# Where the work of a two-layer graph kernel stands: adjacency maxima out of the second sweep, a new order in the gates' stage, filters read once

## The chip, the cores and the metric

The kernel runs on one core of a Trainium2 chip. The metric is the device time of one execution in microseconds (us), lower is better. Its engines are PE (TensorE matmul, with weight loads listed apart as PEld), DVE (VectorE), ACT (ScalarE), POOL (GpSimd) and SP (SyncE, which issues all DMAs here). Each has its own instruction queue, worked in order; semaphores tie them together.

## The reference, cut to what matters

There are 64 graphs, each with 256 nodes of 256 channels, and a 256x256 adjacency of zeros and ones.

```python
h = relu(layernorm(x))
# layer 0, with xc = transpose(h)
c = relu(bn1(conv1d(xc, conv1_w)))                 # 1 tap
x_conv = relu(bn2(conv1d(c, conv2_w, pad=8)) + xc)  # 17 taps, 256 x 256 channels
s = h @ w_se.T + b_se                               # 3 values a node
A = exp(-|s_n - s_m|^2) * adj
x_nmp = A @ relu(h @ w_msg.T + b_msg)
gi = concat(x_conv, x_nmp) @ w_ih.T + b_ih ; gh = h @ w_hh.T + b_hh
r, z = sigmoid(gi_r + gh_r), sigmoid(gi_z + gh_z)
x1 = x + (1 - z) * tanh(gi_n + r * gh_n) + z * h
# layer 1, with h2 = relu(layernorm(x1))
out = x1 + relu(h2 @ W[:256] + (adj @ h2) @ W[256:] + bias)
```

## The kernel before

All matmuls of the main work take float16 operands, each value split in a high and a low part and multiplied in three passes. ACT makes the high part, DVE the low one. The splits need powers of two as scales, which come from the largest values and norms of the inputs. The convolution of 17 taps is done in the frequency domain. The kernel has four stages, one after another.

**Preparation** (`convolution_weights`). The filters of `conv2_w` become spectra. They are read twice: once as `conv2_w` (two DMAs of 2176 KB into `wnat`) for the norm of each output channel, L350 on DVE and L321 on ACT, and once as `conv2_tiles`, 37 tiles of 7 output channels, each tile a block of 119 partitions (channel in the tile, tap) by 256 (three DMAs, `CHUNKS`, L251). The first tile DMA waits for the first half of `wnat`, the second for the other half. Once all norms are there, a tile is scaled and split (even pairs of tiles by ACT L316 and DVE L357, odd pairs by POOL L304 to L309), multiplied on PE (L467, 6 matmuls), and its spectrum is split from PSUM into SBUF by ACT (L335) and DVE (L430).

**First sweep** (`convolution`, 66 slots `q`). A slot takes the graphs through a pipeline: DVE takes statistics (L989) and normalises (L1001), PE turns (L1219), ACT and DVE split (L904, L1007), PE multiplies with `conv1_w` (L1230), DVE adds the bias (L1017), ACT and DVE split (L911, L1022), PE transforms (L1244), ACT and DVE split the spectrum (L922, L1029). SP loads an `x` and stores `x_normed` and `h_turned`. In slots 1 to 11 ACT also negates a block of filters (L934), and SP stores the filters in slots 0 to 11 (`store_filters`). From slot 18 on three quarters of a main unit are worked in as well: a unit is 12 matmuls of 512 columns (L1271), a split by ACT (L928) and DVE (L1034) into one of three buffers `ysb`, and a store of 256 KB (L710).

**Second sweep** (same function, 60 units `u`). The main units only, three PSUM banks and three `ysb` buffers deep. Around them, at fixed `u`: all 64 adjacencies are loaded by SP (L761, `load_adj`, 256 KB each, two buffers in `xin`) and reduced to their maxima by DVE (L1070, `adj_max`) by the plan `ADJ_AT`; filters are loaded again and negated (u below 14); two loads of 3072 KB bring spectra back (L738, `load_bins`, before the loop and at u = 11); `place_sides` and `turn_sides` at u = 26 to 36; the weights of the gates are loaded at u = 36 (L765 to L771), squared, summed, scaled and split.

**Gates** (`gates`, 65 slots of one graph). PE runs, for graph t: `distances`, `messages`, `first_h(0)`, `first_conv_rz(0)`, `weighted`, `first_conv_n(0)`, `inverse(t+1)`, `gates_second(0)`, then `turn2(t-1)`, `first_h(1)`, `layer1(t-1)`, `first_conv_rz(1)`, `first_conv_n(1)`, `neighbours(t-1)`, `gates_second(1)`. Nearly all of these are L1557. DVE, ACT and POOL follow in hand-written orders. `weighted_low` (DVE L1649) releases `gates_second(0)`; `norm2` (DVE L1760) releases `turn2` (PE L1771); `finish` adds and rectifies the output.

In the code below, `then` waits for the instruction that it wraps.

## Time and profile before

| what | value |
|---|---|
| median of 3 runs | 1932.36 us (1928.71 to 1933.15) |
| the profiled execution's own time | 1935.05 us |
| its span | 1932.8 us |
| PE busy | 1785.4 us, 92% |
| DVE busy | 1531.6 us, 79% |
| ACT busy | 841.0 us, 44% |
| DMA | 245.55 MB, mean 127 GB/s |
| chain that ended last | PE 36%, DVE 23%, ACT 5% |

Busy shares are means over stages with different limits, so the stages have to be read one at a time. "Idle before" in a row is time in which the engine of that row stood still, with what ended it.

### The profile page before, as it was taken

What the parts mean: (1) busy time and instruction counts of PE and PEld (TensorE: products, weight loads), DVE (VectorE), ACT (ScalarE), POOL (GpSimd) and SP (SyncE); (2) the same over time, 40 slices, a digit from 0 to 9 for tenths busy, and PEclk for the clock granted to TensorE, in tenths of its full rate; (3) what the DMA queues carried; (4) which work ended last, traced back from release to release, by engine and by line L of the source; (5) the groups of instructions that cost most, each with busy time, mean ns of one, the idle gap of its engine ahead of it and who ended that gap; (6) DMA issues with size and microseconds to landing.
All of it is one profiled execution on the core that took longest, in us unless ns stands there. A gap on an engine that the chain in (4) does not pass through costs nothing.

```text
span 1932.8 us, 36810 instructions
## 1 busy us (share of the span) xinstructions
PE 1785.4 (92%) x12477; PEld 1167.3 (60%) x12478; DVE 1531.6 (79%) x3386; ACT 841.0 (44%) x1489; POOL 439.1 (23%) x616
## 2 busy tenths in 40 slices
PE   2778999977779999999999999999999999999997
PEld 1566777732334666666666666666666666666664
DVE  4899999944544788888888888888888888888886
ACT  3664544432233444444444444444444444444442
POOL 3521111100001222222222222222222222222221
PEclk9899999998989999999999999999999999999998
DMA  6376676578684223222232222322223222232320
GB/s 190 108 277 231 220 267 201 193 261 278 190 276 138 76 73 100 79 90 90 72 103 77 91 89 72 103 76 94 86 72 106 74 96 84 73 106 72 97 83 17
DMA packets 172018, 245.55 MB, mean 127 GB/s; under 512 B 14428, under 2 KB 110675, under 8 KB 171210
## 3 DMA queue, kind: packets, MB, share of 16 engines
q1 hardware_dynamic: 171960, 244.81, 38.6%
q8 instruction: 33, 0.54, 0.1%
q14 instruction: 25, 0.20, 0.0%
HBM read 154.57 MB, written 90.18 MB: 127 GB/s over the span
## 4 chain that ended last, share of the span: by engine, by line
PE 36%; DVE 23%; ACT 5%; issue 4%; DVEq 1%; POOL 0%; POOLq 0%
PE ps_rz L1557 16%; PE ps_l L1557 12%; PE ps_n L1557 6%; ACT big L1702 2%; ACT big L1597 2%; DVE big L1693 2%; DVE big L1592 2%; DVE big L1627 2%; DVE big L1649 2%; DVE big L1601 2%; DVE big L1584 2%; DVE big L1736 2%; DVE big L1710 1%; PE ps_d L1771 1%; DVE big L1740 1%
## 5 line engine op out<-in xcount | busy, mean ns | idle before, releaser
L1557 PE MATMUL ps_rz<-big 128*128 128x512 f16 x2304 | 561.2, 380 | 12.0 <-DVE big L1649 9.6
L1557 PEld LDWEIGHTS ps_rz<-big 128*128 128x128 f16 x2304 | 220.1, 98 | 223.5 <-DVE big L1649 20.8
L1271 PE MATMUL m_ps<-big 128*128 128x512 f16 (+1 forms) x1152 | 280.9, 384 | 45.4 <-DVE ysb L1034 42.9
L1557 PE MATMUL ps_n<-big 128*128 128x256 f16 x2304 | 314.3, 273 | 0.0
L1557 PEld LDWEIGHTS ps_n<-big 128*128 128x128 f16 x2304 | 225.2, 98 | 94.6
L1557 PE MATMUL ps_l<-big 128*128 128x512 f16 (+1 forms) x1536 | 273.1, 328 | 2.9 <-DVE big L1806 1.5
L1727 POOL TENSOR_TENSOR big<-big 128x256 f32<-128x256 f32 x128 | 97.5, 761 | 671.1 <-ACT big L1720 671.1
L1702 ACT ACTIVATE big<-big,w_scale 128x512 f32<-128x512 f32 x128 | 92.0, 719 | 287.0 <-DVE big L1693 287.0
L1271 PEld LDWEIGHTS m_ps<-big 128*128 128x128 f16 x1152 | 112.2, 100 | 159.7 <-DVE ysb L1034 56.0
L1557 PEld LDWEIGHTS ps_l<-big 128*128 128x128 f16 x1536 | 150.1, 98 | 91.9 <-issue 2.7
L1557 PE MATMUL ps_b<-big 128*128 128x256 f16 x1536 | 190.3, 274 | 1.5 <-DVE big L1627 1.5
L1557 PEld LDWEIGHTS ps_b<-big 128*128 128x128 f16 x1536 | 146.6, 98 | 40.4 <-DVE big L1627 23.3
L1693 DVE TENSOR_TENSOR big<-ps_rz,w_bias_rz 128x512 f32<-128x512 f32 x128 | 88.7, 693 | 45.2 <-PE ps_rz L1557 42.5
L1070 DVE TENSOR_REDUCE largest<-xin 128x1 f32<-128x512 f32 x64 | 43.5, 685 | 87.2 <-DMA xin<-in_adj 87.1
L928 ACT ACTIVATE ysb<-m_ps 128x512 f16<-128x512 f32 x96 | 56.8, 592 | 126.3 <-DMA spectra<-ysb 63.9
L1720 ACT ACTIVATE big<-big,w_scale 128x256 f32<-128x256 f32 x128 | 65.3, 510 | 92.3 <-DVE big L1713 92.3
L911 ACT ACTIVATE front<-c 128x512 f16<-128x512 f32 x64 | 40.4, 631 | 140.0 <-DVE c L1017 140.0
L1823 DVE SCALAR_TENSOR_TENSOR big<-ps_l,w_scale,w_bias_out 128x256 f32<-128x256 f32 x128 | 61.7, 482 | 45.2 <-PE ps_l L1557 45.2
L1230 PE MATMUL c_ps<-w1t,front 128*128 128x259 f16 x768 | 96.9, 276 | 0.0
L1644 ACT ACTIVATE big<-ps_b 128x512 f16<-128x512 f32 x64 | 38.2, 597 | 123.7 <-PE ps_b L1557 123.7
L1527 ACT ACTIVATE big<-ps_s,cvec 128x256 f32<-128x256 f32 x128 | 65.2, 559 | 57.7 <-PE ps_s L1516 57.7
L1034 DVE SCALAR_TENSOR_TENSOR ysb<-m_ps,ysb 128x512 f16<-128x512 f32 x96 | 65.7, 685 | 30.9 <-ACT ysb L928 30.4
(239 smaller groups left out, 2874.4 us busy)
## 6 DMA issues: line engine op xcount, KB each, us to landing
spectra<-ysb SPq DMA_DIRECT2D x96, 256.0 KB, 2.6
big<-spectra SPq DMA_DIRECT2D x64, 384.0 KB, 3.4
xin<-in_x SPq DMA_DIRECT2D x64, 256.0 KB, 3.2
x_normed<-front SPq DMA_DIRECT2D x64, 256.0 KB, 3.4
h_turned<-front SPq DMA_DIRECT2D x64, 256.0 KB, 2.5
xin<-in_adj SPq DMA_DIRECT2D x64, 256.0 KB, 3.1
big<-h_turned SPq DMA_DIRECT2D x64, 256.0 KB, 3.2
big<-in_adj SPq DMA_DIRECT2D x64, 256.0 KB, 3.6
```

Of the source, the lines that this page charges most:

```text
L928: act.activation(ysb[:, m % 3, :, 0, :], m_ps[m % 3][:, :].rearrange("p (r o) -> p r o", r=2), ACT.Copy, scale=2.0 ** Y_EXP).then_inc(y_hi ...
L1034: dve.scalar_tensor_tensor(out=ysb[:, m % 3, :, 1, :], in0=m_ps[m % 3][:, :].rearrange("p (r o) -> p r o", r=2), scalar=2.0 ** Y_EXP, in1= ...
L1070: dve.tensor_reduce(largest[:, j:j + 1], xin[:, j % 2, :, :].rearrange("p h d -> p (h d)"), axis=AXIS.X, op=ALU.max, apply_absolute_value= ...
L1230: last = pe.matmul(c1_ps[:, t, 0:D + SE], ht[:, f % 2, dl, kh, t * P:t * P + P], w1t[:, wl, kh, 0:D + SE], start=(kh == 0 and n == 0), sto ...
L1271: last = pe.matmul(dest, x_, w_, start=n == 0, stop=n == 11, skip_group_check=True)
L1527: act.activation(conv_y[:, oh, :], ps_s[:, oh * N:oh * N + N], ACT.Identity, scale=cvec[:, 4 + oh:5 + oh], bias=cvec[:, 6 + oh:7 + oh]).th ...
L1557: last = pe.matmul(dest, stationary(dl), moving(wl), start=start and n == 0, stop=stop and n == 2, **kw)
L1693: dve.tensor_tensor(sum_rz[:, i, :], ps_rz[i][:, :], w["bias_rz"][:, :], ALU.add).then_inc(S["rz_added"], 1)
L1702: act.activation(tanh_rz[:, i, :], sum_rz[:, i, :], ACT.Tanh, scale=w["scale"][:, 8:9]).then_inc(S["rz_tanh"], 1)
L1720: act.activation(new[:, i, :], pre_n[:, i, :], ACT.Tanh, scale=w["scale"][:, 10:11]).then_inc(S["n_tanh"], 1)
L1727: pool.tensor_tensor(x_new[:, i, :], xin[:, p, i, :], new[:, i, :], ALU.add).then_inc(S["x_new_done"], 1)
L1823: dve.scalar_tensor_tensor(out=out_sum[:, i, :], in0=ps_l[i][:, 0:D], scalar=w["scale"][:, 11:12], in1=w["bias_out"][:, :], op0=ALU.mult, ...
```

## The change

The maxima of the adjacency leave the second sweep. In slot q of the first sweep SP loads adjacency q (256 KB, into the two bias tiles that are not yet in use), and ACT sums the absolute values of adjacency q - 1 along its rows with `accum_out`, in place, at the end of its slot. The sums take the place of the maxima in the scale. `load_bins` is cut into 12 parts a set, one at each u from 10 to 33. The last stored spectra are waited for at the start of the gates' stage, not at the end of the second sweep, and `load_late` is issued at u = 56.

In the preparation `conv2_w` is no longer read. The squares of a tile's rows are summed by ACT (two tiles of three) or DVE, a small matmul with a table of ones adds up the taps, and DVE makes the scales of a chunk of tiles; there are five chunks, and their first load is the first DMA. ACT and DVE split 7 pairs of tiles, POOL 12 (before 10 and 9). PSUM is used three tiles deep, before four.

In the gates' stage `neighbours(t-1)` comes after `gates_second(t, 1)`; `gate_sums(t, 1)` ends DVE's slot t instead of beginning slot t + 1; `finish` is cut in `out_row` and `finish`, both one slot later; `weighted_low` comes before `adj_split_low`; there is one more slot.

```diff
-CHUNKS = (range(0, 6), range(6, IN_NEG), range(IN_NEG, NT))
+CHUNKS = (range(0, 6), range(6, 12), range(12, IN_NEG), range(IN_NEG, 28), range(28, NT))
...
+def rows_table():
+
+    rows = TAPS * OT
+    out = np.zeros((P, rows + H * P + H * NT), np.float32)
+    for r in range(rows):
+        o = r // TAPS
+        out[r, o * TAPS:(o + 1) * TAPS] = 1.0
+    for n in range(H * P):
+        t, o = divmod(n, OT)
+        out[o * TAPS, rows + n] = 1.0
+        out[n % P, rows + H * P + n // P * NT + t] = 1.0
     return out
...
+                def load_chunk(c):
+                    ts = CHUNKS[c]
+                    sp.dma_start(raw(ts[0], len(ts)), tiles_d[:, ts[0] * D:(ts[-1] + 1) * D]).then_inc(loaded_tiles[c], 16)
+
+                load_chunk(0)
+                sp.dma_start(table[:, :], table_d).then_inc(loaded_rows, 16)
                 sp.dma_start(small[:, :, :], a["channel_values"]).then_inc(loaded_small, 16)
...
-                for h in range(H):
-                    sp.dma_start(wnat[h], wnat_d[h]).then_inc(loaded_w2[h], 16)
...
-                sp.wait_ge(loaded_w2[0], 16)
-                for c, ts in enumerate(CHUNKS):
-                    if c == 1:
-                        sp.wait_ge(loaded_w2[1], 16)
-                    sp.dma_start(raw(ts[0], len(ts)), tiles_d[:, ts[0] * D:(ts[-1] + 1) * D]).then_inc(loaded_tiles[c], 16)
+                load_chunk(1)
+                for c in range(2, len(CHUNKS)):
+                    sp.wait_ge(loaded_tiles[c - 2], 16)
+                    load_chunk(c)
...
+                def chunk_squares(c):
+                    act.wait_ge(loaded_tiles[c], 16)
+                    for t in CHUNKS[c]:
+                        if t % 3 == 1:
+                            continue
+                        act.activation(part(0, t), raw(t), ACT.Square,
+                                       accum_out=row_square[0:ROWS_T, t:t + 1]).then_inc(squares_act, 1)
+
+                chunk_squares(0)
                 tile_high(0)
+                chunk_squares(1)
                 tile_high(2)
...
                 for b, pair in enumerate(PAIRS):
-                    if b % 2 == 1 and b + 3 < len(PAIRS):
+                    if b and b + 3 in TOGETHER:
...
+                    if b in (1, 3, 5):
+                        chunk_squares(b // 2 + 2)
+                    if b == 3:
+                        act.wait_ge(w1_turned, 1)
...
+                def chunk_squares(c):
+                    dve.wait_ge(loaded_tiles[c], 16)
+                    for t in CHUNKS[c]:
+                        if t % 3 != 1:
+                            continue
+                        dve.tensor_tensor_reduce(out=part(1, t), in0=raw(t), in1=raw(t), scale=1.0, scalar=0.0, op0=ALU.mult,
+                                                 op1=ALU.add,
+                                                 accum_out=row_square[0:ROWS_T, t:t + 1]).then_inc(squares_dve, 1)
+
...
+                def chunk_scale(c):
+                    lo, hi = CHUNKS[c][0], CHUNKS[c][-1] + 1
+                    dve.wait_ge(sums_made, c + 1)
+                    then(dve.tensor_scalar(row_norm[0:ROWS_T, lo:hi], pz[3][0:ROWS_T, 1, D + lo:D + hi], 1e-30, None,
...
+                    dve.reciprocal(row_scale[0:ROWS_T, lo:hi], row_power[0:ROWS_T, lo:hi]).then_inc(scales_ready, 1)
...
                 for b, pair in enumerate(PAIRS):
-                    if b % 2 == 1 and b + 3 < len(PAIRS):
+                    if b == 1:
+                        chunk_scale(1)
+                        scale_chain()
+                    if b == 2:
+                        scale_w1()
+                        chunk_squares(2)
+                    if b == 3:
+                        chunk_scale(2)
+                        halve_se()
+                    if b == 4:
+                        chunk_squares(3)
+                    if b == 5:
+                        halve_w1()
+                        chunk_scale(3)
+                    if b == 6:
+                        chunk_squares(4)
+                    if b == 7:
+                        chunk_scale(4)
+                    if b == 10:
+                        channel_values()
+                    if b and b + 3 in TOGETHER:
                         tile_low(b + 3)
...
+                def chunk_sums(c):
+                    lo, hi = CHUNKS[c][0], CHUNKS[c][-1] + 1
...
+                    pe.wait_ge(squares_act, hi - (hi + 1) // 3)
+                    pe.wait_ge(squares_dve, (hi + 1) // 3)
+                    pe.matmul(pz[3][0:ROWS_T, 1, D + lo:D + hi], same, row_square[0:ROWS_T, lo:hi], start=True, stop=True,
+                              skip_group_check=True).then_inc(sums_made, 1)
...
-                    if b % 2 == 1:
-                        pe.wait_ge(low_pool, b // 2 + 1)
+                    if b in BY_POOL:
+                        pe.wait_ge(low_pool, BY_POOL.index(b) + 1)
...
-                            pe.wait_ge(w_low, t - 3)
+                        if b in TOGETHER:
+                            pe.wait_ge(low_dve, 2 * TOGETHER.index(b) + t % 2 + 1)
+                        if t >= 3:
+                            pe.wait_ge(w_low, t - 2)
...
+                    if b == 0:
+                        largest_sums()
+                        chunk_sums(1)
+                    if b in (2, 4, 6):
+                        chunk_sums(b // 2 + 1)
+                    if b == 3:
+                        turn_w1()
+                    if b == 9:
+                        pick_powers()
...
+        adj_in = [w[n][:, :] for n in ("bias_rz", "bias_n")]
...
-                def load_bins(g):
...
+                def load_bins(g, k):
+                    if k == 0:
+                        sp.wait_ge(main_done, HALF_UNITS * (groups - 1 + g))
+                        sp.wait_ge(xb_stored[g], 16 * XB_PARTS)
+                    part = X_SET // XB_PARTS
+                    lo = X_AT[g] + k * part
+                    sp.dma_start(big[:, lo:lo + part], xb_d[g][:, k * part:(k + 1) * part]).then_inc(xb_loaded[g], 16)
+
+                def load_adj(j):
+                    if j >= 2:
+                        sp.wait_ge(adj_seen, j - 1)
+                    sp.dma_start(adj_in[j % 2], adj_d[j]).then_inc(adj_loaded[j % 2], 16)
...
+                    if q < graphs:
+                        load_adj(q)
...
-                load_bins(0)
+                sp.wait_ge(adj_seen, graphs)
                 load_biases()
...
-                    if u == HALF_UNITS - 1:
-                        load_bins(1)
-                    for j in adj_steps(u + 1):
-                        load_adj(j)
+                    if 10 <= u < 34:
+                        load_bins((u - 10) // XB_PARTS, (u - 10) % XB_PARTS)
...
-                    if u == 42:
-                        sp.wait_ge(adj_seen, graphs)
+                    if u == 40:
...
-                for i in range(3):
-                    sp.wait_ge(y_stored[i], 16 * (len(MAIN) // 3))
-                early.load_late(sp)
+                    if u == 56:
+                        sp.wait_ge(weights_low, len(PARTS))
+                        early.load_late(sp)
...
+                def adj_sum(j):
+                    act.wait_ge(adj_loaded[j % 2], 16 * (j // 2 + 1))
+                    act.activation(adj_in[j % 2], adj_in[j % 2], ACT.Abs,
+                                   accum_out=largest[:, j:j + 1]).then_inc(adj_seen, 1)
...
+                    if 0 <= q - 1 < graphs:
+                        adj_sum(q - 1)
...
-                def adj_max(j):
-                    dve.wait_ge(adj_loaded[j % 2], 16 * (j // 2 + 1))
-                    dve.tensor_reduce(largest[:, j:j + 1], xin[:, j % 2, :, :].rearrange("p h d -> p (h d)"), axis=AXIS.X,
-                                      op=ALU.max, apply_absolute_value=True).then_inc(adj_seen, 1)
...
-                    for j in adj_steps(u):
-                        adj_max(j)
...
+        def out_row(dve, t, p, i):
+            ready(dve, "out_done", t, i + 1, H)
+            dve.scalar_tensor_tensor(out=out_sum[:, i, :], in0=ps_l[i][:, 0:D], scalar=w["scale"][:, 11:12],
+                                     in1=w["bias_out"][:, :], op0=ALU.mult,
+                                     op1=ALU.add).then_inc(S["out_added"], 1)
...
+                    slot(j * 2 + p, p, True, True, True, True)
+            slot(graphs - 2, 0, True, True, True, True)
+            slot(graphs - 1, 1, True, True, True, False)
+            slot(graphs, 0, True, True, False, False)
+            slot(graphs + 1, 1, True, False, False, False)
...
+                for i in range(3):
+                    sp.wait_ge(early.y_stored[i], 16 * (2 * HALF_UNITS * graphs // GROUP // 3))
...
                     if prev:
-                        gate_sums(dve, t - 1, 1 - p, 1)
                         gate_new(dve, t - 1, 1 - p, 1)
                     if cur:
                         attention(dve, t, p)
@@ -1920,15 +1999,21 @@
                     if prev:
                         x1_rows(dve, t - 1, 1 - p, 1)
                         x1_stats(dve, t - 1, 1 - p, 1)
+                    if old:
+                        out_row(dve, t - 2, p, 0)
                     if cur:
+                        weighted_low(dve, t, p)
                         adj_split_low(dve, t, p)
-                        weighted_low(dve, t, p)
+                    if old:
+                        out_row(dve, t - 2, p, 1)
                     if prev:
                         norm2(dve, t - 1, 1 - p)
                     if cur:
                         gate_sums(dve, t, p, 0)
                     if prev:
                         h2_split_low(dve, t - 1, 1 - p)
+                    if old:
+                        finish(dve, t - 2, p)
                     if cur:
                         gate_new(dve, t, p, 0)
                         x1_rows(dve, t, p, 0)
@@ -1937,8 +2022,8 @@
                         passed_low(dve, t - 1, 1 - p)
                     if nxt:
                         conv_split_low(dve, t + 1, 1 - p)
-                    if prev:
-                        finish(dve, t - 1, 1 - p)
+                    if cur:
+                        gate_sums(dve, t, p, 1)
 
...
                     if cur:
                         first_conv_rz(pe, t, p, 1)
                         first_conv_n(pe, t, p, 1)
+                    if cur:
+                        gates_second(pe, t, p, 1)
                     if prev:
                         neighbours(pe, t - 1, 1 - p)
-                    if cur:
-                        gates_second(pe, t, p, 1)
```

## Rows read from the trace of the kernel before

**Rows 1.** Busy time by stage: stretch and length, PE, PEld, DVE, ACT, POOL, PEclk, DMA share, GB/s

```profile
0.00:79.20 79.20, 39.72 (x234) 25.02 (x234) 51.86 (x99) 42.47 (x63) 40.67 (x66) 0.96 0.42 130
79.20:397.00 317.80, 288.67 (x2224) 221.09 (x2224) 305.01 (x803) 156.00 (x303) 57.12 (x133) 0.98 0.66 227
397.00:620.40 223.40, 174.46 (x803) 76.68 (x804) 103.92 (x180) 67.18 (x100) 11.99 (x31) 0.92 0.70 237
623.40:1932.80 1309.40, 1282.59 (x9216) 844.47 (x9216) 1070.84 (x2304) 575.36 (x1024) 329.25 (x385) 0.99 0.27 84
```

**Rows 2.** Waits of the second sweep, 397 to 623.5 us: total, times, longest

```profile
DVE largest L1070 <- DMA xin<-in_adj: 87.1, 50, 13.5
ACT ysb L928 <- DMA spectra<-ysb: 63.9, 17, 12.9
...
PE m_ps L1271 <- DVE ysb L1034: 42.9, 20, 9.4
...
ACT big L934 <- DMA big<-wb: 26.8, 12, 10.4
```

**Rows 3.** PE in order of time, late in the second sweep: start, length

```profile
582.39 36.67 PE L1271 MATMUL m_ps<-big 128*128 128x512 f16 x168
```

**Rows 4.** The end of the second sweep in order of time

```profile
619.73 0.69 DVE L1034 SCALAR_TENSOR_TENSOR ysb<-m_ps,ysb 128x512 f16<-128x512 f32 x1 [1.18 <-ACT ysb L928]
622.54 0.34 SPq L1383 DMA_DIRECT2D big<-x_normed  x1
...
623.48 1.76 PE L1516 MATMUL ps_s<-big 128*128 128x96 f16 x18 [4.41 <-PEq L691]
```

**Rows 5.** One slot of the first sweep with `negate`, in order of time

```profile
110.01 0.66 DVE L1007 SCALAR_TENSOR_TENSOR front<-turn_ps,front 128x512 f16<-128x512 f32 x1
...
111.30 0.63 ACT L911 ACTIVATE front<-c 128x512 f16<-128x512 f32 x1 [1.61 <-DVE c L1017]
...
111.84 0.85 ACT L922 ACTIVATE big<-x_ps 128x384 f16<-128x384 f32 x2
...
112.58 1.06 ACT L934 ACTIVATE big<-big 128x1024 f16<-128x1024 f16 x1
...
113.52 0.60 ACT L904 ACTIVATE front<-turn_ps 128x512 f16<-128x512 f32 x1
...
114.44 0.66 DVE L1007 SCALAR_TENSOR_TENSOR front<-turn_ps,front 128x512 f16<-128x512 f32 x1
```

**Rows 6.** The first sweep up to its slot 13, columns as in rows 1

```profile
79.20:140.00 60.80, 41.54 (x340) 34.48 (x341) 55.86 (x155) 33.44 (x59) 12.53 (x30) 0.92 0.77 274
```

**Rows 7.** A later slot, with a main unit

```profile
334.90 0.60 ACT L904 ACTIVATE front<-turn_ps 128x512 f16<-128x512 f32 x1
...
336.71 0.66 DVE L1007 SCALAR_TENSOR_TENSOR front<-turn_ps,front 128x512 f16<-128x512 f32 x1
```

**Rows 8.** Groups of the preparation, 0 to 79.2 us: busy, mean ns, idle before

```profile
L430 DVE TENSOR_TENSOR big<-pz,big 128x672 f16<-128x672 f32 x36 | 30.1, 889 | 3.6 <-ACT big L335 3.5
L335 ACT ACTIVATE big<-pz 128x672 f16<-128x672 f32 x36 | 28.7, 857 | 4.3 <-PE pz L467 3.5
...
L316 ACT ACTIVATE big<-big,row_scale 119x256 f16<-119x256 f32 x10 | 4.4, 495 | 10.5 <-DMA big<-in_conv_tiles 10.5
...
L321 ACT ACT_TABLE_LOAD x1 | 1.3, 1283 | 0.7 <-PEq L2033 0.7
...
L321 ACT ACTIVATION_READ_ACCUMULATOR big<-big 128x1 f32 x2 | 0.4, 186 | 0.0
```

**Rows 9.** DMA queue, 26 to 56 us: packets, MB, share of 16 engines

```profile
q1 hardware_dynamic: 481, 3.84, 42.7%
```

**Rows 10.** A group on PE in the gates' stage: busy, mean ns, idle before

```profile
L1557 PE MATMUL ps_rz<-big 128*128 128x512 f16 x2304 | 561.2, 380 | 12.0 <-DVE big L1649 9.6 <-DVE big L1550 0.5
```

**Rows 11.** One slot of the gates' stage in order of time

```profile
1214.99 0.68 DVE L1649 SCALAR_TENSOR_TENSOR big<-ps_b,big 128x512 f16<-128x512 f32 x1
...
1217.69 0.60 PE L1771 MATMUL ps_d<-ident,big 128*128 128x128 f32 x4
```

297 lines of the change are left out of this document (136 added, 161 removed).

## The prediction

> **What bounds the kernel now.** I read the busy time by stage first [rows 1]. There are four stages: preparation to 79.2 us, first sweep to 397, second sweep to 620.4, gates from 623.4. In the gates PE is busy 1282.59 of 1309.40 us, so that stage is bound by PE and can give back at most its idle 27 us. In the first sweep DVE is busy 305.01 of 317.80 us and PE 288.67: DVE bounds it, PE is close behind, and ACT has half of its time free (156.00). In the second sweep no engine is full: PE 174.46, DVE 103.92, ACT 67.18 of 223.40 us, at a DMA share of 0.70. A stage in which nobody is full waits for transfers or in a chain, so the list of waits comes next [rows 2]. There DVE stood 87.1 us in front of adjacency loads, ACT 63.9 us in front of stores from `ysb`, and PE 42.9 us in front of DVE's split. The order is the clue: PE waits for DVE, and DVE waits for an adjacency. ACT's stores are late because DVE, which fills their low half, is late. What the stage does without adjacencies shows in its last 36.67 us, where PE ran 168 main matmuls, 14 units, in one piece [rows 3]: 2.62 us a unit. There are 60 units, so the floor is some 157 us and the stage took 223.4.
>
> **Second sweep: the main term.** Removed are 64 loads and 64 reductions. PE's work is 59 units of 2.62 us (154.5), one unit of half width (1.3), and 83 further matmuls (803 less 720 [rows 1]): 64 turns a quarter as wide and 19 sums. At the per-matmul time of [rows 3], 0.218 us for 512 columns, they are between 0 and 18 us; by their widths I take 6. The last split adds 0.60 + 0.69 us behind PE. That is 163.1. I add 3.6 for two places where a transfer can still be late. At the start ACT waited up to 10.4 us for a filter block [rows 2], since 3072 KB of bins stood ahead of it; these now go in parts from u = 10 on, and only the biases (0.77 MB) stay ahead. At u = 36 the weights (3072 KB) still stand ahead of the stores of the next units, where ACT's wait of 12.9 us is [rows 2]. Three `ysb` buffers and three banks let PE run on until six units after unit 36, 15.7 us, and by that row the store behind the weights lands about 13 us after them, with four adjacencies in the same queue that now go. I take no more than 3.6 for both. So 166.7 in place of 223.4: **-56.7**. Bounds: -60.3 without the allowance; with each stall as long as PE's longest, 9.4 us [rows 2], 163.1 + 18.8 = 181.9, or -41.5. The other loads fit: up to u = 11 a unit moves 0.79 MB in 2.62 us, 300 GB/s.
>
> **End of the second sweep.** DVE's last split ends at 620.42, SP issues `load_late` only at 622.54, behind the last store's landing, and PE starts at 623.48 [rows 4]. After the change SP has only the store's issue left. I take **-2.1**, the distance from 620.42 to 622.54. The wait reappears on SP at the start of the gates, ahead of the loads for graph 1, which PE needs some 12 us later: hidden.
>
> **First sweep: what is added.** Each slot gets a load of 256 KB on SP, behind `load_x`, and one ACT instruction of 512 elements with an accumulator read, at the end of ACT's slot. What stands behind it on ACT is `negate` and then L904, the split that DVE's L1007 needs. The slot in [rows 5] shows the room: L904 ends at 114.12 and L1007 starts at 114.44, in DVE's own order, 0.32 us later. From ACT's spacing (L911 to L922 0.54 us) and 0.186 us for an accumulator read [rows 8] the new instruction takes 0.73 to 0.82 us. So L904 ends at about 114.86, 0.44 us after DVE wants it, and as the whole loop L1007, L1017, L911, L922, L934, L904 turns on itself, each slot with a `negate` grows from 4.43 to 4.87 us. That is 11 x 0.44 = 4.8 us. In slots without `negate` (0.94 us by spacing) the same loop is shorter by that and the addition lies in ACT's free time. In a later slot L904 ends at 335.50 and L1007 starts at 336.71 [rows 7]: 1.21 us of room against 0.82. DMA: the first slots reach a share of 0.77 at 274 GB/s [rows 6], which is 356 GB/s at share 1. A slot up to 11 would carry 1.57 MB, 322 GB/s over 4.87 us; slots with spectra to park (18 to 29, 34 to 45) 1.5 MB in 4.95 us, 305 GB/s. Both fit below 356 but with little left, so I add 2.2 us. Sum **+7**. Bounds: +2 if ACT's instruction is cheaper in line; +28 if the 0.44 us comes in all 64 slots. SP waits for ACT's sum ahead of the store of `x_normed`, about 1 us later than now; DVE wants that buffer two slots on.
>
> **Preparation.** The tile rows come slowly: 3.84 MB in 30 us, 42.7% of 16 engines [rows 9]. All 37 tiles are 4.5 MB, so at 128 GB/s the last chunk lands 35 us after the first begins, near 39. Chunk 0 (0.73 MB) lands near 8. After it come four squares on ACT (0.495 + 0.186 us each, by the tile's ACT row and the read [rows 8]), the sums and scales (2 us), chunk 1's squares near 18, and DVE begins on filters near 20. From there DVE has 37 x 0.889 us [rows 8] = 32.9, and 10 low halves, 8 squares, four scale chains and the moved small work, some 18: 71. ACT from 19 on has 37 x 0.857, 17 squares (11.6), 10 high halves (5.0) and 1: 68. They are nearly equal and have their extra work at different pairs, with PSUM only three tiles deep, so I add 4: end at 75 for 79.2, **-4**. Bounds -12 (PE's, ACT's and DVE's waits of now all gone) and +3 (the sums of both engines meet badly).
>
> On the slow tile rows the Trainium skill, "DMA: Bandwidth & Descriptors", section "Why a DMA increments its semaphore by 16 and not by 1", says that a DMA uses the largest number of engines up to 16 that divides its slowest dimension; for 119 rows this is 7. By that rule, the trace agrees: 7 of 16 is 43.8%, beside 42.7% in [rows 9]. It speaks against this change in so far as the read that stays is the one on 7 engines. On 16 the tiles would land in 15 us and the stage's end would still be DVE's.
>
> **Gates.** Nothing is added or removed; PE's sum stays. PE idled 12.0 us before ps_rz, 9.6 of them for `weighted_low`, L1649 [rows 10]. With `gates_second(1)` ahead of `neighbours`, DVE gets the sums of row 1 some 1.3 us earlier (12 matmuls of 256 columns at half of 0.218 us), and `weighted_low` no longer follows `adj_split_low`: that wait goes. Smaller ones of the same kind are about 1 us. At the very end the tail of the last graph starts 1.3 us earlier. What is late next is `norm2`: behind L1649 (start 1214.99, spacing 0.6) now come `adj_split_low` 0.65, `out_row` 0.43 and `norm2` 0.74, ending near 1217.4, and PE turns at 1217.69 [rows 11], some 0.2 us earlier after the change. It fits by 0.1 us. I take **-11**; bounds -13 and +6, if `norm2` came 0.3 us late in 62 slots.
>
> **Sum.** -56.7 - 2.1 + 7 - 4 - 11 = -66.8. Against the profiled execution's own 1935.05 us that is 1868.3. That execution lies 2.7 us above the median of the runs; from the median 1932.36 the forecast is **1865.6 us**.
>
> **Rivals.**
> A. The second sweep keeps its stalls, at the weights and the first filters: -41.5 in place of -56.7, 1881. For it: the 12.9 us wait and SP's one queue. Against: PE's reserve of six units.
> B. The sum on ACT or the load delays every slot of the first sweep: +28 in place of +7, 1887. For it: DVE and PE are both nearly full there. Against: the 1.21 us of room in [rows 7].
> C. The gates gain nothing or lose, `norm2` taking the place of `weighted_low`: 1877 to 1883. For it: the margin of 0.1 us.
> D. Other side: the function that takes absolute values is not in ACT's loaded table, so that each of 64 slots has two table loads of 1.283 us [rows 8]. ACT's loop in later slots, 4.65 us with a unit and the sum, becomes 7.2 for 4.95, and in the first 7.4 for 4.43: 53 x 2.3 + 11 x 3.0 = 155, less the 74 that the rest gives: 2013. It decides from 74/64 = 1.15 us more a slot. Against: the preparation mixes Copy and Square with one table load in all. The Trainium skill, "ScalarE: Activation LUTs", section "Table sets: the hidden batching unit", lists abs among the cheap functions that every set holds; no run here shows it yet.
>
> **Chances.** Forecast (within its terms' small errors, 1855 to 1875) 0.58; A 0.14; B 0.12; C 0.12; D 0.02; a mix of small mishaps 0.02. The range goes from 1847, where every term has its good bound (-60.3 - 2.1 + 2 - 12 - 13 = -85.4), to 1889, a little above B, and so takes in A, B and C. A measurement of this kernel tells 0.3%, 5.8 us, from no change. Faster by more than that 0.97, within it 0.01, slower 0.02.
>
> **What would show it.** Right: the second sweep lasts 165 to 170 us with PE at 2.62 us a unit and hardly a wait of DVE; eleven waits of L1007 for L904 of some 0.4 us early in the first sweep and none later; a preparation that ends near 75; PE's wait for L1649 gone. Wrong: PE waits for `ysb` after u = 36, slots of more than 5 us throughout the first sweep, PE waiting before L1771, or table loads between the sums.

## The result, and the profile after

The changed kernel takes **1905.01 us**, the median of 4 runs (1900.41 to 1907.59), against 1930.53 us (1928.65 to 1933.15) for the kernel before in the same job. The ratio is 0.9864, 95% interval 0.984 to 0.9889. It is faster by 1.4%, the interval excludes 1, but by 25 us and not by the forecast 67: 1905 lies above the range's end of 1889. The profiled execution took 1906.06 us, its span is 1904.3.

Busy time by stage after the change (columns as in [rows 1]):

```profile
0.00:82.60 82.60, 49.75 (x244) 28.65 (x244) 57.86 (x132) 46.91 (x103) 51.72 (x75) 0.88 0.22 71
82.60:403.00 320.40, 288.54 (x2224) 221.09 (x2224) 306.07 (x803) 190.40 (x431) 57.11 (x133) 0.99 0.82 277
403.00:568.10 165.10, 161.36 (x803) 75.81 (x804) 64.21 (x117) 66.90 (x100) 12.01 (x31) 1.00 0.65 220
569.00:1904.30 1335.30, 1292.33 (x9216) 844.60 (x9216) 1103.21 (x2304) 573.94 (x1024) 310.92 (x384) 0.99 0.27 82
```

Set against [rows 1], a loss stands beside every gain:

| stage | before | after | measured | forecast |
|---|---|---|---|---|
| preparation, to the first sweep's first DVE instruction | 79.28 | 82.67 | +3.4 | -4 |
| first sweep | 317.8 | 320.4 | +2.6 | +7 |
| second sweep | 223.4 | 165.1 | -58.3 | -56.7 |
| its end, last split to the first matmul of the gates | 3.06 | 0.96 | -2.1 | -2.1 |
| gates | 1309.4 | 1335.3 | +25.9 | -11 |

The two sweeps with their end came out 6 us better than the sum said. The gates are 37 us worse than forecast, and the preparation is 7 us worse. The number of matmuls in the gates is the same, 9216, and PE's busy time rose from 1282.59 to 1292.33 us; the rest is waiting. DVE's busy time rose from 1070.84 to 1103.21 us for the same 2304 instructions. No instruction was added there, so some instruction has become slower: this is the line to follow.

The waits of the gates' stage after the change (total, times, longest), PE's own:

```profile
PE ps_d L1846 <- DVE big L1835: 33.3, 62, 5.3
...
PE ps_rz L1632 <- DVE big L1724: 0.8, 1, 0.8
```

The wait for `weighted_low` (L1649 before, L1724 now) is gone but for 0.8 us; it was 9.6 us in [rows 10]. In its place PE waits in front of `turn2` (L1846, before L1771) for `norm2` (L1835): 61 waits of 0.46 us, one in nearly every slot, and the one of 5.3 us in the last slot, which the kernel before has too (6.6 us). One slot in order of time, DVE, POOL and the two neighbours on PE:

```profile
1213.13 0.69 DVE L1724 SCALAR_TENSOR_TENSOR big<-ps_b,big 128x512 f16<-128x512 f32 x1 [0.80 <-ACT big L1719]
1213.74 0.74 DVE L1659 SCALAR_TENSOR_TENSOR big<-big,w_scale 128x512 f16<-128x512 f32 x1
1214.40 0.48 DVE L1894 SCALAR_TENSOR_TENSOR big<-ps_l,w_scale,w_bias_out 128x256 f32<-128x256 f32 x1
1214.79 1.61 DVE L1835 TENSOR_SCALAR big<-big 128x256 f32<-128x256 f32 x2
1215.10 1.15 POOL L1608 TENSOR_TENSOR big<-big 128x512 f32<-128x512 f32 x1 [2.08 <-ACT big L1602]
...
1216.33 0.68 DVE L1768 TENSOR_TENSOR big<-ps_rz,w_bias_rz 128x512 f32<-128x512 f32 x1
1216.33 1.16 POOL L1612 TENSOR_TENSOR big<-big 128x512 f32<-128x512 f32 x1
...
1216.46 0.66 PE L1846 MATMUL ps_d<-ident,big 128*128 128x128 f32 x4 [0.46 <-DVE big L1835]
```

DVE's queue did what the prediction said: `norm2` starts 1.66 us behind the start of `weighted_low`, forecast 1.68. But the pair takes 1.61 us and not 0.74. In the kernel before, the pair ran from 1215.95 to 1216.69 and POOL's add began at 1216.80, 0.11 us behind it:

```profile
1215.95 0.74 DVE L1760 TENSOR_SCALAR big<-big 128x256 f32<-128x256 f32 x2 [0.27 <-POOL big L1754]
...
1216.80 1.16 POOL L1533 TENSOR_TENSOR big<-big 128x512 f32<-128x512 f32 x1 [0.89 <-ACT big L1527]
```

The list of one line's instructions splits the pair (count, then ns min/median/max); after the change, in the slots at 1214.8 and 1235.4:

```profile
L1835 DVE TENSOR_SCALAR big<-big x4: 407/852/1298, 1214.8 to 1235.7; 128x256 f32<-128x256 f32 x4
```

One of a pair takes 0.41 us as always, the other 1.30. Counted back from the pair's end at 1216.40, the second starts at 1215.10, with POOL's add, and ends 0.15 us behind that add's end. So it looks as if it stood still until POOL was done. `gate_sums` right behind it (L1768), whose first operand comes from PSUM, takes its usual 0.68 us beside POOL's next add, and that add its usual 1.16.

Three explanations are tested below. A: the overlap with POOL's add makes `norm2` long. B: its new place or its operands do. C: PE's new order costs the time.

### The profile page after: what moved, and what is told of

Its sections match the earlier page's. It is cut to its first block, busy times and chain, and to the rows that moved or that the text cites. A ratio compares the mean times of both kernels' runs of the same rounds, so it can differ in the third digit from the quotient of the medians.

```text
span 1904.3 us, 37114 instructions
## 1 busy us (share of the span) xinstructions
PE 1792.0 (94%) x12487; PEld 1170.2 (61%) x12488; DVE 1531.3 (80%) x3355; ACT 878.2 (46%) x1657; POOL 431.9 (23%) x625
## 4 chain that ended last, share of the span: by engine, by line
PE 55%; DVE 10%; ACT 2%; issue 2%; DVEq 0%; POOL 0%; ACTq 0%; POOLq 0%
PE ps_rz L1632 22%; PE ps_l L1632 13%; PE ps_n L1632 9%; PE ps_b L1632 9%; DVE big L1835 5%; DVE big L1659 2%; PE ps_d L1846 2%; ACT big L1719 2%; DVE big L1894 1%; PE ps_d L1641 1%; DVE big L1724 0%; DVEq L1547 0%; ACTq L1552 0%; ACT big L1777 0%; DVE big L1768 0%
## 5 line engine op out<-in xcount | busy, mean ns | idle before, releaser
L1345 PE MATMUL m_ps<-big 128*128 128x512 f16 (+1 forms) x1152 | 268.5, 375 | 4.4 <-DVE big L1110 2.2
L1802 POOL TENSOR_TENSOR big<-big 128x256 f32<-128x256 f32 x128 | 105.3, 823 | 632.8 <-ACT big L1795 632.8
L1768 DVE TENSOR_TENSOR big<-ps_rz,w_bias_rz 128x512 f32<-128x512 f32 x128 | 87.8, 686 | 46.0 <-PE ps_rz L1632 46.0
L1853 ACT ACTIVATE big<-ps_d 128x512 f16<-128x512 f32 x64 | 38.3, 598 | 145.6 <-PE ps_d L1846 145.6
L1608 POOL TENSOR_TENSOR big<-big 128x512 f32<-128x512 f32 x64 | 73.7, 1152 | 133.7 <-ACT big L1602 131.4
L1835 DVE TENSOR_SCALAR big<-big 128x256 f32<-128x256 f32 x128 | 100.8, 831 | 0.3 <-POOL big L1829 0.3
```

Of the source, the lines that this page charges most:

```text
L1345: last = pe.matmul(dest, x_, w_, start=n == 0, stop=n == 11, skip_group_check=True)
L1608: pool.tensor_tensor(conv_x[:, :, :], conv_y[:, :, :], ht[:, p, 0, :, :], ALU.add).then_inc(S["conv_h"], 1)
L1768: dve.tensor_tensor(sum_rz[:, i, :], ps_rz[i][:, :], w["bias_rz"][:, :], ALU.add).then_inc(S["rz_added"], 1)
L1802: pool.tensor_tensor(x_new[:, i, :], xin[:, p, i, :], new[:, i, :], ALU.add).then_inc(S["x_new_done"], 1)
L1835: last = dve.tensor_scalar(h2hat[:, i, :], x1[:, p, i, :], meanvar_b[:, i, 0:1], rstd_b[:, i:i + 1], ALU.subtract, ALU.mult)
```

## Experiments

Totals are medians, and each kernel has a ratio to the kernel before, run on the same chip. The kernel before was between 1934 and 1937 us in these jobs (1930.5 in the first), so kernels are compared by ratio and by the stages of their profiles. The profile is of one execution. "Sweep from" is the first DVE instruction of the first sweep, "gates from" PE's first matmul of the gates, "gates" the rest of the span.

| kernel | us | ratio, interval | sweep from | both sweeps | gates from | gates |
|---|---|---|---|---|---|---|
| before | | | 79.28 | 544.2 | 623.48 | 1309.3 |
| after | 1905.0 | 0.9864, 0.984 to 0.9889 | 82.67 | 486.4 | 569.04 | 1335.3 |
| g_norm2_early | 1862.9 | 0.9622, 0.96 to 0.9644 | 81.03 | 487.3 | 568.30 | 1294.1 |
| g_pool_held | 1859.6 | 0.9606, 0.9584 to 0.9627 | 78.98 | 486.6 | 565.61 | 1292.9 |
| g_norm2_stt | 1912.3 | 0.9878, 0.9853 to 0.9903 | 79.99 | 487.0 | 567.03 | 1344.2 |
| g_old_order | 1878.7 | 0.9703, 0.968 to 0.9725 | 78.29 | 490.6 | 568.93 | 1308.9 |
| s_only | 1870.4 | 0.9671, 0.9655 to 0.9688 | 76.78 | 485.5 | 562.31 | 1304.2 |
| p_old | 1858.2 | 0.96, 0.9584 to 0.9616 | 78.36 | 486.6 | 564.98 | 1294.1 |
| b_depth3 | 1939.5 | 1.0025, 1.001 to 1.0039 | 82.98 | 545.2 | 628.21 | 1309.5 |
| p_alternate | 1859.9 | 0.9615, 0.9597 to 0.9632 | 77.01 | 487.0 | 564.02 | 1293.1 |
| p_best | 1858.1 | 0.9599, 0.9571 to 0.9627 | 75.56 | 488.4 | 563.91 | 1292.7 |
| s_sum_twice | 1874.3 | 0.9686, 0.9645 to 0.9727 | 78.99 | 500.8 | 579.77 | 1292.8 |
| s_bins_whole | 1872.8 | 0.9681, 0.9648 to 0.9713 | 76.84 | 496.5 | 573.38 | 1293.1 |

**g_norm2_early.** One line of DVE's order moved:

```diff
                         weighted_low(dve, t, p)
+                    if prev:
+                        norm2(dve, t - 1, 1 - p)
+                    if cur:
                         adj_split_low(dve, t, p)
                     if old:
                         out_row(dve, t - 2, p, 1)
-                    if prev:
-                        norm2(dve, t - 1, 1 - p)
```

> The changed kernel with one instruction pair moved on VectorE's queue: norm2 stands right behind weighted_low instead of behind adj_split_low and out_row(1). It then starts at about 13.74 on the slot's clock of the changed kernel's trace (rstd2 is ready at 13.02), 1.36 us ahead of GpSimd's conv_add (15.10). Theory A (VectorE's norm2 is slow because GpSimd's 128x512 add runs beside it): the pair takes 0.74 us again instead of 1.61, TensorE's wait in front of turn2 (0.46 us in each of 62 slots, 0.67 with the drained pipe) is gone, the slot falls from 20.57 to about 19.9 us and the gates' stage from 1335 to about 1294; total about 1863. Rival B (norm2 was only late, its duration belongs to the new place of its operands): the pair still takes about 1.6 us but ends at 15.35, ahead of the 15.98 at which turn2 wants it, so the stage falls just the same; the pair's duration in the trace tells A from B. Rival C (TensorE's own new order, neighbours behind gates_second, costs the time): a stage of over 1315, total over 1885.

The gates take 1294.1 us, 41 less than after the change, and PE's wait for `norm2` is the one of 5.3 us in the last slot. The pair is short again, and lies clear of POOL's add:

```profile
1213.65 0.73 DVE L1835 TENSOR_SCALAR big<-big 128x256 f32<-128x256 f32 x2
1215.02 1.16 POOL L1608 TENSOR_TENSOR big<-big 128x512 f32<-128x512 f32 x1 [1.89 <-ACT big L1602]
...
1215.75 0.60 PE L1846 MATMUL ps_d<-ident,big 128*128 128x128 f32 x4
```

That is theory A. B asked for a pair of 1.6 us and C for a stage over 1315; both fall. The next `turn2` starts at 1235.64: a slot of 19.89 us in place of 20.57.

**g_pool_held.** DVE's order stays; POOL waits instead:

```diff
                     if nxt:
+                        if prev:
+                            ready(pool, "h2hat_done", t - 1)
                         conv_add(pool, t + 1, 1 - p)
```

> The changed kernel with VectorE's queue as it is, and one wait more on GpSimd: conv_add of the next graph waits until norm2 is done. Nothing is moved on VectorE, the overlap alone is taken away. Theory A (overlap slows norm2): the pair takes 0.74 us at its old place (14.79 to 15.53), ahead of the 15.98 at which turn2 wants it; slot about 19.9 us, stage about 1294, total about 1863; conv_add starts about 0.4 us later, and the split after it has 8 us to spare. Rival B (position or operands make it 1.6 us long): the pair keeps 1.6 us, the slot stays at 20.57, total about 1905. Rival C (TensorE's order): no change of the total either, though the pair is short.

A wait is added and nothing else, and the kernel gets faster by 2.6% of the time before (ratio 0.9606 for 0.9864). `norm2` stands where it stood, behind `out_row`, and takes 0.73 us:

```profile
1231.00 0.48 DVE L1894 SCALAR_TENSOR_TENSOR big<-ps_l,w_scale,w_bias_out 128x256 f32<-128x256 f32 x1
1231.39 0.73 DVE L1835 TENSOR_SCALAR big<-big 128x256 f32<-128x256 f32 x2
...
1232.37 1.16 POOL L1608 TENSOR_TENSOR big<-big 128x512 f32<-128x512 f32 x1 [2.75 <-DVE big L1835]
1232.44 0.60 PE L1846 MATMUL ps_d<-ident,big 128*128 128x128 f32 x4
```

Over the stage, ns min/median/max of the instruction: here, and in g_norm2_early all the same; after the change a maximum three times as long.

```profile
L1835 DVE TENSOR_SCALAR big<-big x126: 402/408/414, 614.7 to 1844.2; 128x256 f32<-128x256 f32 x126
```

```profile
L1835 DVE TENSOR_SCALAR big<-big x124: 405/410/1300, 618.1 to 1873.3; 128x256 f32<-128x256 f32 x124
```

This run takes the overlap away and keeps DVE's order and the operands. It is the one that shows the cause.

**g_norm2_stt.** `norm2` in another form, same place, same neighbour:

```diff
-                last = dve.tensor_scalar(h2hat[:, i, :], x1[:, p, i, :], meanvar_b[:, i, 0:1], rstd_b[:, i:i + 1],
-                                         ALU.subtract, ALU.mult)
+                last = dve.scalar_tensor_tensor(out=h2hat[:, i, :], in0=x1[:, p, i, :], scalar=meanvar_b[:, i, 0:1],
+                                                in1=spread_rstd, op0=ALU.subtract, op1=ALU.mult)
```

`spread_rstd` is the rstd repeated along the row, a second operand in SBUF.

> The changed kernel with norm2 written as scalar_tensor_tensor (rows minus mean, times the rstd repeated along the row) in the same place, beside the same conv_add. Scalar_tensor_tensor of 128x256 f32 takes 0.43 us each in all rows of the stage, also where GpSimd works. Theory A in its narrower form (it is the fast form of tensor_scalar, 0.37 us each alone, that suffers beside GpSimd, and the forms that take 0.43 don't): the pair takes about 0.8 us, ends at 15.6, the wait is gone, total about 1863. Theory A in a wide form (every form of VectorE's is slowed beside a GpSimd add): the pair takes 1.3 to 1.6 us, total 1895 to 1905. Rival B: as the wide form.

The narrow form of theory A fell. The run was not faster than the changed kernel: by ratio the two are not told apart (0.9878 for 0.9864, the intervals overlap), and the gates' stage took 8.9 us more, with a pair of 1.77 us:

```profile
1217.38 1.77 DVE L1836 SCALAR_TENSOR_TENSOR big<-big 128x256 f32<-128x256 f32 x2
1217.69 1.18 POOL L1608 TENSOR_TENSOR big<-big 128x512 f32<-128x512 f32 x1 [2.08 <-ACT big L1602]
```

The wide form, every instruction of DVE's, is too wide: `gate_sums` reads PSUM and SBUF and stays at 0.68 us. My reason for the narrow one was false, too. I wrote that this form takes 0.43 us everywhere in the stage. The kernel before shows `x1_rows` beside POOL's `add_new`:

```profile
1221.04 0.43 DVE L1733 SCALAR_TENSOR_TENSOR big<-big 128x256 f32<-128x256 f32 x1 [0.58 <-ACT big L1720]
1221.08 0.88 POOL L1727 TENSOR_TENSOR big<-big 128x256 f32<-128x256 f32 x1 [1.89 <-ACT big L1720]
1221.50 0.74 DVE L1736 SCALAR_TENSOR_TENSOR big<-big 128x256 f32<-128x256 f32 x1
```

L1736 takes 0.74 us here and 0.43 in the same slot at 1212.87, where POOL is idle. L1733 began 0.04 us ahead of POOL and kept its 0.43. So the row that gave this effect away stood in the trace of before. POOL pays too when it is second. Its `add_new` takes 0.64 us at 1210.38, beside a DVE instruction with an operand from PSUM (L1618), and 0.88 when it starts behind L1733; over the stage, ns min/median/max:

```profile
L1727 POOL TENSOR_TENSOR big<-big x114: 635/759/883, 707.9 to 1844.5; 128x256 f32<-128x256 f32 x114
```

The rows fit one rule: of a DVE instruction and a POOL instruction whose operands all come from SBUF, the one that starts first runs and the other waits for it. The Trainium skill, "SBUF — State Buffer", section "Who interferes with whom", states this rule: a DVE instruction with two SBUF inputs contends with a GpSimd instruction that reads SBUF, and so does one in a fast two-port form (`tensor_scalar` is named as able to enter it); they share a port pair, the first one holds it for the whole instruction, and a DVE instruction with at most one SBUF input outside those forms is left alone. All the rows above agree with it: 0.41 against 1.30 us, 0.43 against 0.74, and an unchanged 0.68 with one input in PSUM. What no run here separates is the port from any other cause of the same exclusion.

**g_old_order.** The new orders of the gates undone on DVE, PE and SP (the wait for `y_stored` stays on SP).

> The changed kernel with the gates' orders of the kernel before on VectorE, TensorE and SyncE (gate_sums(1) at the head of the next slot, adj_split_low ahead of weighted_low, neighbours ahead of gates_second(1), finish in one piece), and the rest of the change kept. If the parts add up, the stage takes 1309 us again as before, in place of 1335, and the total is about 1879. If the preparation or the sweeps of the changed kernel leave the stage something worse (loads late, tables in other banks), it stays above 1320 and the total above 1890.

The stage takes 1308.9 us, as before (1309.3), and PE's wait for `weighted_low` is back. The total of 1878.7 is the forecast 1879.

```profile
PE ps_rz L1632 <- DVE big L1724: 11.2, 60, 1.0
```

The new orders by themselves thus cost 26 us, and with the overlap gone they bring 15 to 16. (Both sweeps took 490.6 us here, 4 more than in g_pool_held with the same code; half of that lies in the first 12 slots, see p_best.)

**s_only.** The kernel before with the change in `convolution` and the wait for `y_stored` alone.

> The kernel before with the sweeps' part of the change alone: adjacencies in the first sweep as row sums, bins in parts, weights in the background, y_stored waited for in the gates' stage. Preparation and gates are those of before. Theory (the sweeps' terms are right by themselves): first sweep +3, second sweep -58, boundary -2, so the span is 1932.8 - 57.7 = 1875 and the ratio 0.970. Rival (the parts lean on each other, for instance the new preparation brings the first sweep its start, or the new gates' order hides the store's end): more than 6 us away from 1875.

Both sweeps and the boundary take 485.5 us for 544.2, -58.7 where the changed kernel has -57.8. The span is 1866.5 rather than 1875; of these 8.5 us less, 2.5 are a preparation that ended early (76.78) and 5 are gates of 1304.2 us. Of these 5, 3.3 lie in the slots: in the kernel before every second one takes 20.17 instead of 20.05 us, here nearly all take 20.05. Another 0.7 lie ahead of the first `turn2`, where PE's granted clock in the first 5 us of the stage was 1.00 here and 0.50 in the kernel before, and 1.1 behind the last one. Why the slots differ stays open. In the rival's letter it is over 6 us off, but not where the rival said: the parts of the sweeps do not lean on the others.

**p_old.** g_pool_held with the old preparation.

> The version with GpSimd held (1859.6 us) with the preparation of the kernel before put back: filters read twice, norms by rows of channels, PSUM four tiles deep. The profiles of five kernels with the new preparation begin the first sweep at 82.67, 81.03, 78.98, 79.99 and 78.29 us (mean 80.2), the one of before at 79.28. Theory (the new preparation gives nothing at all): the old one begins the sweep at 79 to 80 and the total is 1857 to 1861. Rival (the new one costs the 3.4 us that the two first profiles show): total 1856 or less. Rival (it brings the 4 us that were forecast, and the profile of before was a lucky one): sweep from 83 on, total 1863 or more.

1858.2 against 1859.6 us (0.96 and 0.9606): no difference. Preparation that is the same code begins the sweep at 82.67, 81.03, 78.98, 79.99, 78.29, 78.99 and 76.84 us in seven profiles (mean 79.5), the old one at 79.28, 76.78 and 78.36 (mean 78.1). So the +3.4 us of the profile after the change is mostly scatter. The step is worth +1.4 us between the means, with 5.8 us between the ends of the seven; the forecast -4 is not there.

**b_depth3.** The kernel before with three PSUM tiles for the filters:

```diff
-            return pz[t % 4][:, :, 0:SPAN * OT].rearrange("p k (e o) -> p k e o", o=OT)[:, :, :, 0:WIDTHS[t]]
+            return pz[t % 3][:, :, 0:SPAN * OT].rearrange("p k (e o) -> p k e o", o=OT)[:, :, :, 0:WIDTHS[t]]
-                        if t >= 4:
-                            pe.wait_ge(w_low, t - 3)
+                        if t >= 3:
+                            pe.wait_ge(w_low, t - 2)
-                                last = pe.matmul(pz[t % 4][:, kh, 0:SPAN * OT],
+                                last = pe.matmul(pz[t % 3][:, kh, 0:SPAN * OT],
```

> The kernel before with one thing of the new preparation: PSUM three tiles deep for the filters (pz[t % 3], TensorE waits for w_low of t - 3 in place of t - 4). Nothing else. Theory D (the ring PE, ScalarE, VectorE turns on too few buffers, and this is what the new preparation pays): the sweep begins 3 to 6 us later than 79.28, total about 1937. Rival E (depth does not matter, VectorE's own work is the bound): at most 1 us later, total as before.

The sweep begins at 82.98, 4.8 us behind the mean of the three old preparations, and the total rises by 0.25% (0.1 to 0.39, or 2 to 7.5 us). Theory D holds. PE's wait for DVE's `w_low` tells the same, first b_depth3, then the kernel before (both to the end of the preparation):

```profile
PE pz L467 <- DVE big L430: 11.9, 14, 4.3
```

```profile
PE pz L467 <- DVE big L430: 3.2, 5, 1.3
```

**p_alternate.** g_pool_held with `TOGETHER = (0, 2, 4, 6, 8, 10, 12, 14, 16, 18)`.

> The version with GpSimd held (1859.6 us, its first sweep begins at 78.98; mean of five profiles of this preparation 80.2) with pairs 6, 12 and 16 taken from GpSimd: TOGETHER has ten pairs, GpSimd nine, as in the kernel before. VectorE and ScalarE get six half tiles more each (6 x 0.52 and 6 x 0.50 us), GpSimd has 12 us less. Theory E (VectorE's own work bounds the stage): begin of the sweep 3 us later, near 83. Theory F (VectorE's instructions are stretched beside GpSimd's, row_power's 128x2 at 1.14 us in place of 0.23 and so on, and this is what the stage pays): the stretching falls by a quarter, and the begin moves by less than 1 us or comes earlier.

The sweep begins at 77.01 us, within the scatter of the seven, and the total is 1859.9. Theory E, 83, falls: six more half tiles on DVE, 3 us by the forecast, with 12 us less on POOL, cost nothing that shows. Whether less stretching beside POOL paid for them the scatter hides.

**p_best.** p_alternate with the fourth PSUM tile in use again from tile 23 on.

> The version with nine pairs on GpSimd (1859.9 us, sweep begins at 77.01) with a fourth PSUM tile for the filters from tile 23 on, when the sums and the turned weights in that tile have been read. If the depth of three is what the stage pays (4.8 us for 37 tiles in the kernel before), the last 14 of 37 give back up to 1.8 us: the sweep begins at 75 to 76.5, total 1857 to 1860, and TensorE's waits for w_low behind tile 23 are gone. If the depth matters only in the first tiles, nothing moves.

It begins the sweep at 75.56 us, the earliest of all, but takes 1.3 us longer for the first 12 slots, and ends at 1858.1 us. That is 0.3% or less from g_pool_held, so not told apart from it.

The 1.3 us go with PE's granted clock. All kernels with one sum in the first sweep have the same code in these slots, and the lower the clock, the longer they are:

| kernel | PE's granted clock, slots 0 to 12 | their length |
|---|---|---|
| after, g_norm2_early, s_only, p_old | 0.94 | 54.96 to 55.34 |
| g_pool_held | 0.91 | 55.29 |
| g_norm2_stt, p_alternate, p_best, s_bins_whole | 0.88 | 56.05 to 56.64 |
| g_old_order | 0.85 | 57.25 |

So part of the scatter that the tables show has a name, though not a cause.

**s_sum_twice.** g_pool_held with the row sum of ScalarE done twice:

```diff
+                    act.activation(adj_in[j % 2], adj_in[j % 2], ACT.Abs, accum_out=extra[:, j:j + 1]).then_inc(adj_once, 1)
+                    act.wait_ge(adj_once, j + 1)
                     act.activation(adj_in[j % 2], adj_in[j % 2], ACT.Abs,
                                    accum_out=largest[:, j:j + 1]).then_inc(adj_seen, 1)
```

> The version with GpSimd held (1859.6 us) with ScalarE's row sum of each adjacency done twice in the first sweep: 64 more instructions of 0.63 us with a read of 0.20. Its first sweep (82.6 to 403 in the changed kernel, 320.4 us; 317.8 in the kernel before) tells what a row sum costs where. Theory (ScalarE's loop bounds the slots with negate and has room in the others, as forecast): slots with negate grow by the whole 0.6 to 0.8 us, 12 of them, 8 us; later slots had 1.21 us of room before the change, of which one sum took some 0.8, so the second costs up to 0.4 us in each of 52, up to 21. Sweep 328 to 349 us. Rival (DVE alone bounds the sweep and the +2.7 us have another cause, such as transfers): the sweep stays within 3 us of 320.

Lengths from the starts of the first DVE instruction of slots 0, 12, 45 and 63 in the timelines:

| kernel | slots 0 to 12 | 12 to 45 | 45 to 63 |
|---|---|---|---|
| before | 51.96 | 159.13 | 89.78 |
| after | 55.19 | 159.49 | 88.94 |
| g_pool_held | 55.29 | 159.70 | 88.93 |
| s_sum_twice | 62.16 | 166.11 | 90.15 |

One sum costs 3.2 us in the first twelve slots, which hold the eleven with `negate`, and nothing beyond. The clock is not its cause: 0.94 in these slots after the change, 0.90 before. A second sum costs 6.9 us there, about its own length in each, and now 0.19 us in each of the next 33: the room of the later slots is used up. From slot 0 to 63 the sweep grows by 14.5 us, within the theory's 8 to 29, and the rival, under 3 us, falls. The 6.9 is not the sum's alone, though: PE's granted clock was 0.81 in these slots for 0.91 in g_pool_held, and this kernel has two measured runs only.

**s_bins_whole.** g_pool_held with both sets of bins loaded in one run each, at the start of the second sweep and at u = 11.

> The version with GpSimd held (1859.6 us) with the bins of the second sweep loaded in one run each, at its start and at unit 11, as in the kernel before, in place of a part a unit from unit 10 on. The adjacencies stay out of the second sweep. Theory (the adjacencies' loads and reductions were the whole of the 58 us; the bins stand ahead of the first filters only): the first filter block comes some 8 to 10 us late as in rows 2 (10.4 us), TensorE waits for it since its buffers are full, and the total rises by 3 to 10 us, to 1863 to 1870. Rival (the cut of the bins did a large part of the gain): total over 1872. Rival (TensorE's reserve hides it): within 2 us of 1859.6.

The sweeps take 9.9 us more (496.5 for 486.6), with these waits of the second sweep, PE's from 403 us on and ACT's from 395:

```profile
PE m_ps L1348 <- DVE ysb L1118: 9.2, 5, 5.7
```

```profile
ACT big L1016 <- DMA big<-wb: 11.4, 4, 10.4
```

By the ratio the total rises by 0.75%, some 14 us, of which the profile, of the fastest of the four executions, shows 9.9 in the sweeps. The 10.4 us wait for the first filter block is the one of [rows 2], as the theory said, but the price is at or above its 3 to 10 us: the median of 1872.8 lies with the first rival (over 1872), the profiled execution's 1868.3 with the theory. So 10 to 14 of the 58 us come from cutting the bins and starting them later, and 44 to 48 from the adjacencies and what else left that queue.

## Why the prediction was wrong

**Second sweep: right.** 165.1 us for 166.7. PE was busy 161.36 of it, at a granted clock of 1.00; the same 803 matmuls kept it busy for 174.46 us at 0.92 before [rows 1]. That gain is in the forecast, since its 2.62 us a unit come from a stretch without stalls. PE's waits for DVE sum to 2.1 us, where the forecast allowed 3.6 for late transfers. The stall at the weights came as expected in kind and smaller in effect:

```profile
517.34 1.21 ACT L1007 ACTIVATE ysb<-m_ps 128x512 f16<-128x512 f32 x2 [7.47 <-DMA spectra<-ysb]
...
518.72 2.55 PE L1345 MATMUL m_ps<-big 128*128 128x512 f16 x11 [1.71 <-DVE ysb L1115]
```

ACT stood 7.47 us in front of a store behind the weights, PE's six units of reserve left 1.71 of it. Rival A did not come.

**Boundary: right.** The last split ends at 568.08 and PE starts at 569.04. The wait for the last stores on SP costs nothing that shows.

**First sweep: mechanism right, term oversized.** It grew by 2.6 us for +7. Two sizes were off. A slot with `negate` grew by 0.29 us and not 0.44, and the 2.2 us for transfers did not come, at a DMA share of 0.82. The slot answers to [rows 5]:

```profile
113.00 0.63 ACT L1000 ACTIVATE w_bias_rz<-w_bias_rz 128x512 f32<-128x512 f32 x1
113.52 0.20 ACT L1000 ACTIVATION_READ_ACCUMULATOR w_bias_rz<-w_bias_rz 128x1 f32 x1
113.61 1.05 ACT L1013 ACTIVATE big<-big 128x1024 f16<-128x1024 f16 x1
114.56 0.59 ACT L978 ACTIVATE front<-turn_ps 128x512 f16<-128x512 f32 x1
115.18 0.69 DVE L1088 SCALAR_TENSOR_TENSOR front<-turn_ps,front 128x512 f16<-128x512 f32 x1 [0.23 <-ACT front L978]
```

The sum takes 0.61 us of ACT's time by spacing (113.00 to 113.61), not 0.73 to 0.82. Less the 0.32 us of room that the forecast read in [rows 5], that is 0.29 us a slot, and 3.2 us in eleven: the whole growth, with nothing left for transfers. There is no table load between the sums, so rival D is out; rival B too.

**Preparation: the step that failed is "PSUM only three tiles deep, so I add 4".** Start and work were right: DVE began on the filters at 21.75 (forecast 20), and was busy for 51.1 of the 60.3 us from 22.00 to 82.30 (forecast 51). It stood still for 9.2 us, not 4. PE waited for DVE's `w_low` 7.8 us in eight pieces, and ACT 17.7 us for PE where it had waited 3.5 before [rows 8]. b_depth3 puts the price of the third tile alone, without the mixed work, at 4.8 us by the profile, as much as the whole allowance or more.

The forecast has no term for PE's clock either. The granted clock over the preparation was 0.96 in the three old ones and 0.87 to 0.91 in the seven new ones, lowest in the two that end last. One stretch of the profile after the change: the first twelve matmuls ran at a granted clock of 1.00, the next twelve, behind a wait of 3.17 us, at 0.78.

```profile
58.58 1.87 PE L539 MATMUL pz<-q_sb,big 119*128 119x336 f16 x12 [0.21 <-DVE big L485]
63.62 2.52 PE L539 MATMUL pz<-q_sb,big 119*128 119x336 f16 x12 [3.17 <-DVE big L485]
```

How the rest splits between the mixed work, PE's clock and POOL's presence stays open, under a scatter of 6 us.

**Gates: the step that failed is "`norm2` 0.74", and with it "It fits by 0.1 us".** This is the step that broke the forecast. The removal of the wait for `weighted_low` was right, and so was the time at which `norm2` starts. Its duration, 0.74 us, was taken from a place where POOL was idle, and moved to one where POOL is busy. The trace of before could have said so: by the forecast's own times `norm2` would run to 1217.4, and POOL's add (L1533) starts at 1216.80. Held there, it ends 3.27 us behind the start of `weighted_low` instead of 2.42, and PE stops in 61 slots. Undisturbed, in g_pool_held, it fits by 0.3 us (1232.12 to 1232.44). PE's recorded wait is 0.46 us, but the slot is 0.68 longer (20.57 for 19.89). Of the other 0.22, 0.06 is in `turn2` itself (0.66 us for 0.60); about 0.17 is that without a wait it starts that much ahead of the recorded end of the group before it (1231.79 + 0.82 against 1232.44). In g_norm2_stt it is the same 0.22: a wait of 0.62 us and slots of 20.73. 61 x 0.68 = 41.5 us, which is what g_norm2_early and g_pool_held give back in the stage (41.2 and 42.4). With `norm2` in time, the stage gains 15 to 16 us, 4 to 5 more than forecast.

Rival C named the place and the victim, and had 12 in 100. Its price, 0.3 us late in 62 slots for +6 at most, came from the margin in the queue only. No case had a longer duration in it, and so the range's end had none.

## What to carry over

When an instruction of VectorE is moved, look at what GpSimd does at the new place, and take its duration from rows with the same company: a `tensor_scalar` or `scalar_tensor_tensor` on SBUF beside a GpSimd add took up to three times as long. A wait that keeps GpSimd off the critical instruction can pay well; here one was worth 2.6%. And read a stage's own scatter over several profiles before you put a few microseconds down to an edit.

## What was not expected of the hardware

VectorE and GpSimd exclude each other by whole instructions where both work from SBUF: `norm2`'s second half took 1.30 us in place of 0.41 beside an add of 1.15, `scalar_tensor_tensor` 1.38 in place of 0.48 (the list of g_norm2_stt's line), while `tensor_tensor` with one operand in PSUM stayed at 0.68. A short stop of PE costs more than its record: 0.46 us waited, 0.68 lost. And the same code of the preparation ended at any point between 76.84 and 82.67 us, with PE's granted clock at 0.87 to 0.91.
